# An unrolled rebuild of a fused attention and expert kernel: front by chunks, three stack buffers, experts beside the last slot

## The reference, cut to what matters

```
s = first_attention(xn)      # 16 heads of 8, causal softmax, layernorm of the
                             # result with gamma and beta, times Wo
h = rmsnorm(xn) * ln1        # second network: attention with rotation
q, k, v = h@Wq+bq, h@Wk+bk, h@Wv+bv   # 16 q heads, 4 shared k and v heads
q, k = rmsnorm(rope(q)), rmsnorm(rope(k))         # per head of 8
o = softmax(causal(q k / sqrt(8))) v
y = xn + (o * sigmoid(o@Wg+bg)) @ Wo + bo
h2 = rmsnorm(y) * ln2
e = argmax(h2@Wr+br)         # one of 8 experts for each token
y = y + ((u1 * sigmoid(u2)) @ W2[e] + b2[e]),  u1, u2 = h2@W1[e]+b1[e]
out = x + s * silu(y)
```

## Time and profile before

| what | value |
|---|---|
| median of 3 runs | 921.66 us (920.74 to 926.14) |
| profiled execution | 916.86 us |
| its span, first to last instruction | 915.1 us |
| TensorE busy | 784.3 us, 86% |
| ScalarE busy | 600.5 us, 66% |
| VectorE busy | 552.1 us, 60% |
| POOL busy | 227.0 us, 25% |
| mean granted TensorE clock | 0.946 of full speed |

### The profile page before, as it was taken

The page is one execution under the profiler, slowest core; times in us unless marked ns, Lnnn a source line. Parts: engine busy times, 40 slices in busy tenths (PEclk is TensorE's granted clock), DMA queues, the critical chain, the costliest instruction groups (busy, mean ns, idle before and its releaser), DMA issues.

```text
span 915.1 us, 30078 instructions
## 1 busy us (share of the span) xinstructions
PE 784.3 (86%) x11912; PEld 361.1 (39%) x11912; DVE 552.1 (60%) x1095; ACT 600.5 (66%) x771; POOL 227.0 (25%) x438
## 2 busy tenths in 40 slices
PE   3712869999997999999799999999999999889990
PEld 2302224444442444444344444443443434424660
DVE  7894336676643666666156666656999547405524
ACT  2424657778867887887678878877565776664331
POOL 7383130211120112011201121023101303262533
PEclk8866889999999999999999999999999999989995
DMA  3435450030033001202310020024000311030003
GB/s 70 138 103 164 149 111 3 3 106 3 6 106 107 3 3 37 72 3 61 109 49 3 3 92 16 3 84 130 2 3 2 113 33 46 14 97 8 33 26 101
DMA packets 39450, 50.59 MB, mean 55 GB/s; under 512 B 10476, under 2 KB 29712, under 8 KB 39304
## 3 DMA queue, kind: packets, MB, share of 16 engines
q1 hardware_dynamic: 38056, 45.99, 16.9%
q0 software_dynamic: 1248, 2.57, 0.8%
HBM read 36.82 MB, written 11.42 MB: 53 GB/s over the span
## 4 chain that ended last, share of the span: by engine, by line
PE 67%; DVE 12%; ACT 6%; issue 6%; SPq 5%; DMA 2%; POOL 1%; ACTq 0%; DVEq 0%; POOLq 0%
PE PS L1057 22%; PE PS L1042 21%; PE PS L1017 11%; ACT PR L891 6%; DVE MP L1370 4%; PE PS L1196 3%; PE PS L1073 2%; SPq L564 2%; SPq L558 2%; PE PS L1216 1%; PE PS L1021 1%; DVE CROW L1307 1%; DVE OT L1389 1%; DMA q_parts<-QA 1%; PE PS L1195 1%
## 5 line engine op out<-in xcount | busy, mean ns | idle before, releaser
L891 ACT ACTIVATE PR<-PS 128x1024 f32<-128x1024 f32 (+3 forms) x640 | 537.2, 895 | 195.4 <-PE PS L1042 192.7
L1370 DVE TENSOR_REDUCE MP<-PS 128x1 f32<-128x512 f32 (+3 forms) x640 | 366.7, 607 | 170.8 <-PE PS L1017 87.2
L1042 PE MATMUL PS<-QA,KA 128*32 128x512 bf16 (+3 forms) x5120 | 348.6, 354 | 45.2 <-DMA QA<-CROW 20.5
L1057 PE MATMUL PS<-PR,VA 128*32 128x512 f32 (+3 forms) x2560 | 295.8, 536 | 14.9 <-POOL PR L783 13.0
L1017 PE MATMUL PS<-MB 72*32 72x512 bf16 (+3 forms) x2560 | 224.4, 351 | 6.4 <-DVE MP L1370 3.5
L783 POOL TENSOR_SCALAR_AFFINE_SELECT PR<-PR 128x256 f32<-128x256 f32 x256 | 102.3, 408 | 474.1 <-ACT PR L891 471.5
L1042 PEld LDWEIGHTS PS<-QA,KA 128*32 128x32 bf16 x5120 | 120.8, 97 | 228.2 <-ACT PR L891 111.6
L1017 PEld LDWEIGHTS PS<-MB 72*32 72x32 bf16 x2560 | 69.6, 95 | 103.2 <-DVE MP L1370 60.8
L1057 PEld LDWEIGHTS PS<-PR,VA 128*32 128x32 f32 x2560 | 72.9, 111 | 55.7 <-POOL PR L783 16.4
L1021 PE MATMUL PS<-CM,IDB 128*32 128x128 bf16 x1024 | 57.9, 221 | 0.2
L1389 DVE COPY OT<-PS 128x512 f32<-128x512 f32 x32 | 21.9, 685 | 54.2 <-PE PS L1057 54.2
(11 more groups left out here) (206 smaller groups left out, 465.9 us busy)
## 6 DMA issues: line engine op xcount, KB each, us to landing
QA<-q_parts SPq DMA_DIRECT2D x96, 96.0 KB
KA<-k_parts SPq DMA_DIRECT2D x96, 96.0 KB
MB<-q_parts SPq DMA_DIRECT2D x48, 96.0 KB
MB<-k_parts SPq DMA_DIRECT2D x48, 96.0 KB
q_parts<-QA SPq DMA_DIRECT2D x8, 384.0 KB, 2.5
k_parts<-QA SPq DMA_DIRECT2D x8, 384.0 KB, 2.7
MB<-in_L_ffn_W SPq DMA_DIRECT2D x1, 2048.0 KB, 9.0
expert_tokens<-ZERO SPq DMA_DIRECT2D x1, 1483.5 KB, 10.0
```

Source lines behind the costliest of these rows:

```text
L891: act.activation(PR[:, tile % RING, :, 0:CH - q0], PS[:, 2 * p:2 * p + 2, 0:CH - q0], ACT.Exp).then_inc(s_ex, 1)
L1042: last = pe.matmul(PS[r:r + STRIP, 2 * p + k, 0:CH - q0], KA[:, b, kb // BPC, 2 * p + k, key:key + STRIP], QA[:, b, c, 2 * p + k, q0:CH], ...
L1057: last = pe.matmul(PS[32 * hh:32 * hh + 32, 6, q0:CH], VA[:, b, kb, hh, :], PR[:, (2 * s + hh // 2) % RING, hh % 2, 0:CH - q0], start=kb = ...
L1370: dve.reduce_max(MP[:, BPC * (HG * (qb // BPC) + hh) + qb % BPC, kc:kc + 1], PS[:, unit_bank(u, peeled), 0:w], AX).then_inc(s_mr, 1)
```

## The change

The program is written out without a loop, and most of it is new:

- *Steps.* Chunks go from first to last, and 128 and 384 queries on the diagonal share one step: 3, 7, 11 and 15 steps, 36 a slot, 288 in all. The number n counts them through all slots; `at(slot, s)` is one.
- *Front by chunks.* Each chunk of 512 tokens goes through norm, projection, rotation, head norm and split by itself. Chunks 0 and 1 and part of 2 come before step 0, the rest and the whole projection of the first attention at fixed steps of slot 0 (`FRONT_AT`). All inverse roots are powers on POOL; that of the heads is 80 columns a chunk (`head_scales`).
- *Stacks.* There are three buffers; maxima read the same stack as the scores, MB is gone; k of the second network is stored once for four heads. Two constant rows take the place of CROW and the ones.
- *Maxima.* Four sets go from step 25 of slot 0 to step 5 of slot 7 (`MAX_SPAN`), and each chunk's shift is handed over by itself.
- *FFN chain.* The output, gate, router and places stand beside slots 5 and 6, by chunks (`FFN_AT`).
- *Experts.* The 23 tiles stand beside slot 7 from its step 8 (`MOE_AT`), one to a step. Both sigmoids are Tanh of the half.
- *Weights* come in three packed arrays made from the inputs' layout (front, late, const), which hold what POOL and TensorE built and turned.
- *End.* TensorE projects the first attention into four banks, and VectorE joins from there.

```diff
+def chunk_steps(c):
+
+    d = BPC * c
+    full = [(c, [(kb, 0, 0)]) for kb in range(d + 1)]
+    return full + [(c, [(d + 1, P, 0), (d + 3, 3 * P, 3 * P)]), (c, [(d + 2, 2 * P, 0)])]
+
+
+STEPS = [s for c in range(NC) for s in chunk_steps(c)]
...
+MAX_SPAN = [(at(0, 25), at(2, 5)), (at(2, 7), at(4, 4)), (at(4, 7), at(5, 28)), (at(5, 29), at(7, 5))]
...
+FRONT_AT = {0: [("X", 3)], 1: [("P", 6), ("P", 7)], 4: [("Q", 2), ("K", 2)], 7: [("Q", 3), ("K", 3)]}
+for c in range(NC):
+    FRONT_AT[10 + 3 * c] = [("AQ", c)]
+    FRONT_AT[11 + 3 * c] = [("AK", c)]
+    FRONT_AT[12 + 3 * c] = [("AV", c)]
+PROLOGUE = [("X", 0), ("P", 0), ("P", 1), ("X", 1), ("P", 2), ("P", 3), ("Q", 0), ("K", 0), ("X", 2), ("P", 4), ("P", 5),
+            ("Q", 1), ("K", 1)]
...
+FFN_AT = {}
+for k in range(NC):
+    n = at(FFN_SLOT, LAST[k]) + LAG + 3
+    FFN_AT[n] = [("O", k)]
+    FFN_AT[n + 2] = [("G", k)]
+    FFN_AT[n + 5] = [("W", k)]
+    FFN_AT[n + 8] = [("H", k)]
+    FFN_AT[n + 10] = [("R", k)]
...
+MOE0 = at(NG - 1, 8)
+MOE_AT = {}
+for k in range((NT + BPC - 1) // BPC):
+    MOE_AT.setdefault(MOE0 - 3 + 4 * k, []).append(("E", k))
+for j in range(NT + 2):
+    MOE_AT.setdefault(MOE0 + j, []).append(("M", j))
...
+            def load(slot, c):
+                b, g = slot % NBUF, SLOT_GROUP[slot]
                 for j in range(PARTS):
-                    sp.dma_start(q[r * j:r * (j + 1), c, :, :].rearrange("p h s -> p (h s)"),
+                    sp.dma_start(QA[r * j:r * (j + 1), b, c, :, :].rearrange("p h s -> p (h s)"),
                                  QP[c][j, g].rearrange("d h s -> d (h s)").unsqueeze(1)
...
+            events = [(at(j - 2, 1), "load", j) for j in range(NBUF, NG)]
+            events += [(n + 1, "shift", k) for n, ws in SHIFT_AT.items() for _, k in ws]
...
+            def power(out_, in_, n, ready, number, done):
+                gp.wait_ge(ready, number)
+                gp.tensor_tensor(out_, in_, MHALF[:, 0:n], ALU.pow).then_inc(done, 1)
...
+            def head_scales(c):
+                if c >= 1:
+                    gp.wait_ge(s_qk, c)
+                power(HS[:, 1, :], HS[:, 0, :], BPC * 20, s_hs, c + 1, s_rr)
...
+            rstd(0)
+            rms(0)
+            rstd(1)
+            rope_second(0)
+            head_scales(0)
+            rms(1)
+            keep_values(0)
+            rstd(2)
+            rope_second(1)
+            head_scales(1)
+            rms(2)
+            keep_values(1)
+            rstd(3)
+            rope_second(2)
+            rms(3)
+            head_scales(2)
+            keep_values(2)
...
+            for n in range(END):
+                if n < N and n % NS in DIAGONAL:
+                    masks(n)
+                if n == 1:
+                    rope_second(3)
+                    head_scales(3)
+                    keep_values(3)
...
+                for p in range(2):
+                    if n < N:
+                        if n >= RING // 2:
+                            act.wait_ge(s_pv, n - RING // 2 + 1)
+                        act.wait_ge(s_sc, 2 * n + p + 1)
...
+                        w = width(n % NS)
+                        ffn = SLOT_GROUP[n // NS] < NKV
+                        act.activation(PR[:, (2 * n + p) % RING, :, 0:w], PS[:, 2 * p:2 * p + 2, 0:w], ACT.Exp,
+                                       **({"bias": QKM[:, 0:1]} if ffn else {})).then_inc(s_ex, 1)
...
+            def expert(j):
+                if j < NT:
...
+                    experts.append(e)
+                    free(("up", j))
+                    read(pe, ("E", j // BPC))
+                    pe.matmul(PS[:, 4, :], TE[:, j, :], B12[:, 0:4 * P], start=True, stop=False)
+                    pe.matmul(PS[:, 4, :], XG[:, j // BPC % 3, j % BPC * P:(j % BPC + 1) * P],
+                              W1S[:, bass.ds(e, 1), :].rearrange("p a n -> p (a n)"),
...
+            def head_norm(c):
+                dve.wait_ge(s_rr, c + 1)
...
+            rope_first(0)
+            head_squares(0)
+            normed(1)
+            head_norm(0)
...
+            evict(1)
+            split(0)
+            split(1)
+            rope_first(1)
+            head_squares(1)
+            normed(2)
+            head_norm(1)
+            statistics(3)
+            evict(2)
+            split(2)
+            split(3)
+            normed(3)
+            rope_first(2)
+            head_squares(2)
+            head_norm(2)
```

More of the change, by code:

```diff
@@ L78, in item_width @@
     return (qb % BPC + 1) * P if kc == qb // BPC else CH
-def spread(steps):
-    def step_time(s):
-        return step_width(s) + 400
-    def item_time(i):
-        return item_width(i) + 64
-    total, work = sum(map(step_time, steps)), HG * sum(map(item_time, range(len(ITEMS))))
-    out, u, done, own = [], 0, 0, 0
-    for n, s in enumerate(steps):
-        own += step_time(s)
-        mine = []
-        while u < UNITS and (n == len(steps) - 1 or done * total < own * work):
-            mine.append((u // HG, u % HG))
-            done += item_time(u // HG)
-            u += 1
-        out.append(mine)
-    return out
@@ new lines, with works @@
+ROUTED = n + 10
+FFN_AT[ROUTED + 2] = [("N", 0)]
+FFN_AT[ROUTED + 4] = [("B", 0)]
+SCATTER = ROUTED + 6
+MOE0 = at(NG - 1, 8)
[4 more added lines that the diff above has]
+    MOE_AT.setdefault(MOE0 + j, []).append(("M", j))
+LN_AT = {}
+for k in range(NC):
+    LN_AT.setdefault(at(NG - 1, LAST[k]) + LAG + 4, []).append(("L", k))
+END = N + LAG + 8
+def works(n):
+    return [w for table in (FRONT_AT, SHIFT_AT, FFN_AT, LN_AT, MOE_AT) for w in table.get(n, ())]
@@ L263, in build @@
+NF = 536
+C_LN1, C_GAMMA, C_BETA, C_LN2, C_BG, C_QN, C_KN = range(7)
+L_WA, L_WO, L_WG, L_BO, L_WR, L_BR = 0, 512, 640, 768, 896, 904
+NL = 912
+K_ID, K_TRI, K_CM, K_EARLIER, K_BEFORE, K_RANK, K_TOK, K_SPARE, K_TILE, K_J, K_OWN = 0, 128, 256, 384, 520, 584, 592, 608, 631, 654, 670
+NK = 678
+def build(nc, x, front, late, const, W1, W2, b1, b2, out):
     with ExitStack() as ctx:
@@ L1001, in max_unit, with free, turn_xn @@
-            def max_unit(i, item, hh, peeled):
+            def free(key):
+                before = BEFORE_USE[key]
+                if before is None:
+                    return
+                if before[0] == "unit":
+                    pe.wait_ge(s_mr, before[1] + 1)
+                elif READER[before] in ("A", "D"):
+                    read(pe, before)
+            def turn_xn(c):
+                pe.wait_ge(s_xn, c + 1)
+                for i in range(BPC):
+                    last = pe.transpose(PS[:, BANK["X", c], i * P:(i + 1) * P], XN[:, BPC * c + i, :], ID)
+                last.then_inc(s_fl, 1)
@@ new lines, in _ @@
+            pe.wait_ge(s_kc, 16)
+            pe.wait_ge(s_cast, 2)
+            for name, k in PROLOGUE:
+                work(name, k)
+            for n in range(END):
+                parts = maxima_at(n)
+                for p in range(2):
+                    if n < N:
+                        scores(n, p)
+                    for unit in parts[p]:
+                        max_unit(unit)
+                if 0 <= n - LAG < N:
+                    values(n - LAG)
+                if ended(n - LAG - 1) is not None:
+                    turn(ended(n - LAG - 1))
+                for unit in parts[2]:
+                    max_unit(unit)
+                for name, k in works(n):
+                    work(name, k)
@@ new lines, in _ @@
+            parts_at = {}
+            for a in range(NA):
+                for c in range(NC):
+                    parts_at.setdefault(maxima_end(a, c), []).append(NC * a + c)
+            for n in range(END):
+                parts = maxima_at(n)
+                for unit in (*parts[0], *parts[1]):
+                    max_unit(unit)
+                if ended(n - LAG) is not None:
+                    copy_out(ended(n - LAG))
+                if ended(n - LAG - 1) is not None:
+                    normalise(ended(n - LAG - 1))
+                for unit in parts[2]:
+                    max_unit(unit)
+                for k in parts_at.get(n, ()):
+                    shift_parts(k)
+                late(n)
+                for name, k in works(n):
+                    work(name, k)
+                if n == at(1, 10):
@@ L1585, in _ @@
[L1585 to L1597 removed]
+                    dve.wait_ge(s_kc, 16)
```

2226 lines of the change are left out of this document (1063 added, 1163 removed).

## The result

The changed kernel takes 946.6 us, the median of four runs (945.9 to 949.6), the one before 923.1 in the same comparison. The ratio is 1.0259, with a 95% interval of 1.0218 to 1.0299: it is slower. The forecast was 885, range 835 to 914.

What follows compares the result with a forecast made beforehand. TensorE was taken to bound the slot pairs, busy 155 of 158 us. Front 173 + middle 566 + slot 7's rest 116 + tail 24 = 879 of span, 881 with 1.8 around it, 885 as median; range 835 to 914.

Steps and rivals of the forecast that it cites:

- Front, 173: Start to step 25 of slot 0: four POOL head-scale powers at 13.2 us, nothing covering them; step 25 at 173 us.
- the rule weighed there: Front: VectorE ops with two SBUF inputs are blocked while POOL reads SBUF; without it 6 us earlier in all.
- The 36 us "worse by that step": Front: step 25 of slot 0 at 173 where the same work would otherwise end near 137.
- Middle, 566: Step 25 of slot 0 to step 5 of slot 7: TensorE's 526.4, FFN chain 13.6, chunk ends 16, places with router 10.
- FFN chain beside slots 5 and 6: per chunk two turns 0.59, gate 1.06: Middle: with as much as the gate for the output and router 0.1, 13.6 us in all.
- every hand-over has a step between: Slot 7: the argument against rival 3, that the experts' chain locks onto the steps.
- Chunk ends, 16: Middle: 26 ends, three short steps where there were four, 0.6 us each instead of 1.0; 16 us, range none to 26.
- Slot 7's rest, 116: Step 5 of slot 7 to last step: TensorE's rest 52.8, 23 experts 55.0, turns 5, chunk ends 3.
- Tail, 24: After the last step: turn to projection 9, VectorE's sums and ops 11, last store and landing 3; 24 us taken.
- the first (cheap power): Rival 1, front: power of 80 columns takes 2 to 3 us, four times 11 fall away, 841 us; chance 0.20.
- the third: Rival 3, slot 7: experts' chain locks onto the steps, each costing TensorE two Exps, 43 us more, 928; chance 0.08.
- The second: Rival 2: short steps and queues take back the loops' cost, standstills being instruction fetching; 913 us; chance 0.12.

Runs made afterwards that it cites:

- the last versions: Four mends combined, with the last set from step 26, four free steps at the places, none in two slot 1 steps; then more units at chunk ends: 870.9, 870.5 us.

## Why the prediction was wrong

Its four stretches, by its own steps:

- **Front, 173: right, 167.5.** The power's price of 13.2 and its place on the path four times came as worked out, and without it step 25 comes 37.8 us earlier, where the forecast had 36. Step 4, forecast at 109, started at 90.2, and it is step 5 that starts at 108.2, with the same wait. What was off is the rule weighed there, which I let decide the queue: the norms of the next chunk did not stand behind the power. The powers start at 18.8, 42.8, 68.0 and 88.0, forecast were 18, 45.7, 74 and 93.4; the last two are early by the 6 us that the rule was said to be worth, though no run takes its part alone. The first scores at 64 came by luck: the second power ends 2.9 us early, and what follows it takes as much longer. The 36 us "worse by that step" hold against the front with cheap roots alone. The kernel before starts its step there at 165.8 and not at 137, since the 42.4 us leave out the stall and its maxima.
- **Middle, 566: failed, 618.4.** Of the 52 us, 25 are the FFN chain and 27 what the next item has. The failed step is the one that begins "FFN chain beside slots 5 and 6: per chunk two turns 0.59, gate 1.06": 13.6 us, TensorE's own time alone. With places and router I had 23.6 for what the run without FFN puts at 49.0. TensorE's work was a little larger, 17.6, since four products of 8 columns for the router take 0.99 and not 0.1. The other 31 are waits and what the clock takes behind them (about 10): product, sum and square in one step, norm and turn in another, each in order on its engine. One step more between them took back 15. The remainder, with the places, is not taken apart by any run. I had asked that question of the experts ("every hand-over has a step between") and not of the FFN chain, for which it is false in the diff. The places' burst itself was well taken: 10 us forecast with the router, 7.7 measured over a usual step.
- **Chunk ends, 16: too small.** The run without FFN takes 569.4 where TensorE's work and turns are 526.4. 43 us remain, against 16 taken and 26 as the outer bound. By the prediction's own prices slots 2 and 3 lose 3.7 and 5.2, and slots 4 to 6 6.5 to 6.7, where the earlier trace rows gave 3.9 a slot for the kernel before. So a short step less at each chunk brought nothing. Slot 1 loses 12 (VectorE's split of the biases and the clock behind it, of which the last versions took 4 back). With the FFN chain in place, about 14 in the middle are VectorE's reductions: I had written off VectorE by its average in a pair while the same rows show it at 88 of 93 us where a set is squeezed into one slot.
- **Slot 7's rest, 116: right in its sum, 119.8, once three waits are gone that it left out; 137.0 with them.** The layernorm's power moved onto POOL, behind the experts' scatters and once behind the masks. The prediction priced that power only in the front, and the last chunk's in the tail: this term was put at nothing, and the runs show 5 us of waits and 12 of clock behind them. The sum's parts were off both ways: without experts the rest takes 69.2, where it had 116 - 55 = 61 with the tokens' turns, and an expert costs 2.2 beside the slot, where it had 2.39.
- **Tail, 24: right, 21.9.**

Of the rivals, the first (cheap power) and the third (steps of 5.8 us with an expert; they take 4.2) did not come. The second came in part: the chunk ends gave back what the loops cost. Nothing points to fetching: "issue" is 3.6% of the chain through slots 2 and 3, and 4.2% in the kernel before from 462 to 619. The kernel came out slower by a way that none of them named.

The prediction said that it would be wrong if TensorE's share in the middle fell under 93%. It did in slots 5 and 6, with 90% and 89%. Over the stretch that was to show 97%, 173 to 740, it is 94%: a matmul at the lower clock counts as busy too, so this share hides the clock, and the sign was a weak one.

What the last step of a chunk waits for is shown in part. It isn't the masks, and it can't be filled with units. The chain through slots 2 and 3 has 10.1% in ScalarE's Exps, the pair of the kernel before 4.6%. At the end of the second chunk of slot 3 ScalarE first stands 0.88 us for scores, then runs six Exps without a gap, and TensorE's next scores wait for those:

```profile
396.91 6.35 ACT L854 ACTIVATE PR<-PS,QKM 128x1024 f32<-128x1024 f32 x6 [0.88 <-PE PS L947]
...
401.31 0.61 PE L947 MATMUL PS<-QA,KA 72*32 72x512 bf16 x8 [0.17 <-ACT PR L854]
```

That fits the 1.8 us that slot 3 gained without the bias. How much of the loss it is, no run tells. It stays open, too, for how long the clock falls after a wait: the same steps took 3.5 us in one profile and 6.6 in another, which is most of why two kernels 5 us apart in one stage can't be told apart in the total.

## What to carry to other kernels

When a chain is moved beside other work, don't price it by the busiest engine's own time: write down for each step which engine waits in order for which within the same step, since every such wait holds back that engine's next piece of the main work. A step more between hand-overs added no work and took 15 us off the middle here. A function that moves to another engine is priced there at its real width (POOL's power went by the column), and a small op that moves to another queue by what stands ahead of it. Before a gain is put down to an edit, take out what the granted clock differs by in stretches that the edit doesn't touch: it was up to 14 us here.

## What the runs showed of the hardware

- POOL's tensor_tensor with pow goes by the column: 1.01 us for 4 columns, 13.15 for 80, so 0.16 a column and 0.37 besides. ScalarE's Sqrt of the same 80 takes 0.27, and a table load 1.28.
- VectorE was not held up by it. During a power of 13.18 us, the small tensor_tensor with both inputs in SBUF took 0.15 us (L1149 at 19.69), as in the chunks that have no such power beside them (149 to 153 ns in all four). The rope's tensor_tensor of 320 columns took 0.69, 0.90 and 1.03 beside POOL's and 0.48 alone (from 14.93 and from 40.05 on). POOL's op beside it ended 0.34, 0.55 and 0.69 after VectorE's had started, so each took the rest of POOL's and its own time alone, less about 0.14. The Trainium skill (SBUF — State Buffer, Who interferes with whom) has the second of two such ops fully blocked. The rope's rows agree with that; for POOL's pow the measurement speaks against it.
- An Exp whose bias is a column operand takes 1110 ns for 1024 columns and 1020 without. The Trainium skill (ScalarE: Activation LUTs, What ACT_TABLE_LOAD costs) has about 93 ns for such an operand; the trace agrees.
- TensorE's granted clock fell to the lower level (1.2 of 2.4 GHz) at 728, within a wait of 7.1 us, at 800 behind one of 3.8, at 834 at the end of one of 2.1, and at 616 behind one of 2.2. Stretches at that level differ between executions of the same steps: 27 us of the middle in the change, 55 in the run with the layernorm's power earlier.
